# The cell scan of an LSTM recurrence writes to PSUM, and one VectorE operation changes places

## The chip, the core and the metric

The kernel runs on one core of a Trainium2 chip. The metric is the device time of one execution in microseconds (us). The core has TensorE (PE in the profile, its weight loads PEld), VectorE (DVE), ScalarE (ACT), GpSimd (POOL) and SyncE (SP, which only issues DMAs here). Each engine runs its own queue of instructions in order; they meet at semaphores. SBUF is the large on-chip memory, PSUM the small one (here 8 banks of 512 float32 columns on 128 partitions) into which TensorE writes its sums.

## The reference

Four stages in a row on x of shape (4, 256, 128): a conditioned hyperbolic block, a causal multi-head attention, an LSTM over the 256 positions, and a feed-forward layer. The change is in the LSTM alone:

```python
def step(carry, xw_t):                     # 256 steps, one after the other
    prev_h, prev_c = carry
    a = xw_t + prev_h @ Wh                 # (4, 128) @ (128, 512)
    i = sigmoid(a[:, :H]); f = sigmoid(a[:, H:2*H]); o = sigmoid(a[:, 2*H:3*H])
    g = tanh(a[:, 3*H:])
    next_c = f * prev_c + i * g
    next_h = o * tanh(next_c)
    return ((next_h, next_c), next_h)
...
x = x + ffn(lstm(x, cond_1024, Wx, Wh, b))
```

A batch has only four sequences, so every step works on 128 partitions (the hidden units) by a few columns (gates times batch).

## The kernel before

**Layout.** All products with the inputs (Wx) are made ahead, for 32 steps at a time: a chunk. There are 8 chunks (`STEPS` is 32). The accumulators of chunk c stand in PSUM bank 6 or 7, by turns (`bank[:, 6 + (t // STEPS) % 2, ...]`), 16 columns for each step: four gates by batch of four. While chunk c is worked off in one of the two banks, the other one lies idle until step 27 of the chunk; in steps 27 to 31 `inputs_of` fills it for chunk c + 1 (`INPUTS_AT`), where its first matmul starts the sums of the bank afresh.

**One step of the recurrence** goes around the engines like this:

1. TensorE adds h of the step before times Wh to the 16 columns: 12 small matmuls at L1783. h is kept as two float16 parts (`h_off`, and `h_low` for what its rounding leaves), and so is Wh (`wha`, `whb`). Eight matmuls take `h_off` (they wait for `h_ready`), the last four take `h_low` (they wait for `hb_ready`).
2. ScalarE takes tanh of the 16 columns out of PSUM (L832, `gates_act`), into a strided buffer in SBUF, `gates`.
3. VectorE makes the new cell state with one scan over 24 columns (L1391, `c_new`). For each batch element the scan runs through 6 positions, and the sixth is c. It writes to `cell_out`, a buffer in SBUF (`small` in the profile's names).
4. ScalarE takes tanh of the four columns of c (L834, `th_act`).
5. VectorE multiplies it by the output gate into `h_off` (L1402, `h_ready`) and makes `h_low` with a second scan (L1404, `hb_ready`), which reads `h_off` and so waits for `h_ready`.

VectorE has three more small operations in each step. L1393 prepares the output gate. L1397, called the guard below, copies c into the operands of the next step's scan with one bit set, so that it can't be zero; it waits for `c_new` and signals `c_kept`. L1408 takes the reciprocal of what the guard wrote (waits for `c_kept`, signals `c_inverse`), and the next scan waits for it.

**What lies beside it.** Attention of the next chunks, the rest of the hyperbolic block's second half and the feed-forward layer of finished chunks are threaded into the same queues behind each step, at steps written out by hand: `PLAN`, `FFN_STEPS`, and the strings `VEC_GAP` (VectorE work between L1393 and the guard), `VEC_REST`, `ACT_REST` and `PE_REST` (work behind the step). None of these tables changes.

Of the kernel before, what the change touches and what calls it, by code (L numbers as in the profile page):

```python
# [23 lines left out]
ALU = mybir.AluOpType  # L24
ACT = mybir.ActivationFunctionType
# [4 lines left out]
I32 = mybir.dt.int32  # L30

B, S, D, H = 4, 256, 128, 16
# [54 lines left out]
STEPS = 32  # L87
# [5 lines left out]
C_SCALE = 2.0 ** -9  # L93
C_LEAST = 2.0 ** -63
C_LEAST_BITS = 0x20000000
CW = 6
# [5 lines left out]
def adaln_attention_lstm_ffn(nc, x, cond, w_q, b_q, w_k, b_k, w_v, b_v, w_o, b_o, w_f1, b_f1, w_f2, b_f2,  # L102
                             w_ada, b_ada, W_dq, W_uq, W_dkv, W_uk, W_uv, W_o, Wx, Wh, b_g, w1, b1, w2, b2, out):
    with ExitStack() as ctx:
        def sb(name, shape, dt=F32):
            return ctx.enter_context(nc.sbuf_tensor(name, shape, dt))

        def ps(name, shape, dt=F32):
            return ctx.enter_context(nc.psum_tensor(name, shape, dt))

        def sem(name):
            return ctx.enter_context(nc.semaphore(name))
# [97 lines left out]
        cell_out = small[:, 0:2 * CW * B // TILES, :].rearrange("p k t -> p (k t)").rearrange("p (k b s) -> p k b s", k=2, b=B)  # L210
        cell_in1, cell_in0, gate_o = gates[:, :, 0], gates[:, :, 1], gates[:, :, 2, :, 0]
        gates_out = [bass.AP(hn, 3 * k * B * CW + 3, [[3 * TILES * H, P], [(B - 1) * CW + 4, 2], [B * CW - 1, 2], [CW, B]]) for k in range(2)]
        h_fac = sb("h_fac", [P, 2, B, 3])
# [10 lines left out]
        bank = ps("bank", [P, 8, 512])  # L224
# [104 lines left out]
        c_new = sem("c_new")  # L329
        o_ready = sem("o_ready")  # L330
        c_kept = sem("c_kept")
        c_inverse = sem("c_inverse")
        th_act = sem("th_act")
# [4 lines left out]
        x_biased = sem("x_biased")  # L338
        y_ready = sem("y_ready")
        stored = [sem("stored_even"), sem("stored_odd")]  # L340

        block = ctx.enter_context(nc.Block())

# [101 lines left out]
        def attending(t):  # L445
            for c in range(1, CHUNKS):
                if PLAN[c]["co"] <= t <= PLAN[c]["ot"]:
                    yield c
# [5 lines left out]
        def feeding(t):  # L454
            for p, t0 in enumerate(FFN_STEPS):
                feed = FEED_LATE if p == LAST - 1 else FEED
                if 0 <= t - t0 <= feed["result"]:
                    yield p, t - t0, feed
# [7 lines left out]
        def go_on(chain, table, t):  # L466
            for _ in range(int(table[t]) if t < len(table) else 0):
                next(chain)

        @block.sync  # L470
        def _(sp):
# [47 lines left out]
            for k in range(2):  # L519
                sp.wait_ge(stored[k], 16 * sum(c % 2 == k for c, _, _ in PIECES))  # L520
# [67 lines left out]
        def _(act):  # L588
# [228 lines left out]
            def gelu(p, fs=range(FC)):  # L817
                c, a, z = PIECES[p]
                if fs[0] == 0:
                    act.wait_ge(ff_mm, p + 1)  # L820
                    if 2 <= p < LAST:
                        act.wait_ge(y_mm, p - 1)
                for f in fs:
                    nc.scalar.activation(gel[:, c % 2, f, a:z], bank[:, c % 2, f * P + a:f * P + z], ACT.Gelu,  # L824
                                         scale=1.0 / A_SCALE, bias=b1s[:, f:f + 1]).then_inc(gel_ready, 1)

            for t in range(S):
                k = t % 2
                src = bank[:, 6 + (t // STEPS) % 2, (t % STEPS) * GW:(t % STEPS + 1) * GW]

                act.wait_ge(gates_mm, t + 1)
                nc.scalar.activation(gates_out[k], src.rearrange("p (u v b) -> p u v b", u=2, v=2), ACT.Tanh, scale=1.0 / A_SCALE).then_inc(gates_act, 1)  # L832
                act.wait_ge(c_new, t + 1)
                nc.scalar.activation(h_fac[:, k, :, 1], cell_out[:, k, :, 5], ACT.Tanh, scale=1.0 / C_SCALE).then_inc(th_act, 1)  # L834
                for c in attending(t):
                    attend(c, t)
                if t == FFN_STEPS[0]:
                    nc.scalar.preload_act_table_set(GELU)
                go_on(second, ACT_REST, t)
                for p, i, feed in feeding(t):  # L840
                    for j in range(2):
                        if i == feed["gelu"][j]:
                            gelu(p, range(2 * j, 2 * j + 2))
# [3 lines left out]
        def _(vec):  # L847
# [14 lines left out]
            V = nc.vector  # L862
# [523 lines left out]
            for t in range(S):  # L1386
                k = t % 2
                vec.wait_ge(gates_act, t + 1)
                if t:
                    vec.wait_ge(c_inverse, t)  # L1390
                V.tensor_tensor_scan(cell_out[:, k].rearrange("p b s -> p (b s)"), cell_in0[:, k].rearrange("p b s -> p (b s)"),  # L1391
                                     cell_in1[:, k].rearrange("p b s -> p (b s)"), 0.0, ALU.mult, ALU.add).then_inc(c_new, 1)
                V.tensor_scalar(h_fac[:, k, :, 2], gate_o[:, k], 1.0, 0.5 * H_SCALE, ALU.add, ALU.mult).then_inc(o_ready, 1)  # L1393
                go_on(second, VEC_GAP, t)
                if t < S - 1:
                    vec.wait_ge(c_new, t + 1)
                    V.tensor_scalar(cell_in0[:, 1 - k, :, 5].bitcast(I32), cell_out[:, k, :, 5].bitcast(I32), C_LEAST_BITS, None,  # L1397
                                    ALU.bitwise_or).then_inc(c_kept, 1)

                vec.wait_ge(th_act, t + 1)  # L1400
                vec.wait_ge(o_ready, t + 1)
                V.tensor_tensor(h_off[:, t, :, 2], h_fac[:, k, :, 2], h_fac[:, k, :, 1], ALU.mult).then_inc(h_ready, 1)  # L1402
                vec.wait_ge(h_ready, t + 1)
                V.tensor_tensor_scan(h_low[:, t].rearrange("p b s -> p (b s)"), h_fac[:, k].rearrange("p b s -> p (b s)"),  # L1404
                                     h_off[:, t].rearrange("p b s -> p (b s)"), 0.0, ALU.mult, ALU.subtract).then_inc(hb_ready, 1)
                if t < S - 1:
                    vec.wait_ge(c_kept, t + 1)
                    V.reciprocal(cell_in0[:, 1 - k, :, 3], cell_in0[:, 1 - k, :, 5]).then_inc(c_inverse, 1)  # L1408
                for c in attending(t):
                    attend(c, t)  # L1410
                go_on(second, VEC_REST, t)
                if t in BIASED:
                    c = BIASED.index(t)
                    if c == 0:
                        vec.wait_ge(ld_b2, 16)
                    go(V.tensor_tensor(x_tb[:, c, :], x_tb[:, c, :], b2_rows, ALU.add), x_biased)
                for p, i, feed in feeding(t):
                    if i == feed["result"]:
                        result(p)
# [3 lines left out]
        def _(pe):  # L1423
# [266 lines left out]
            def first_inputs(c, gs, t0, t1):  # L1690

                acc = bank[:, 6 + c % 2, :].rearrange("p (t g b) -> p t g b", g=4, b=B)
                for g in gs:
                    ins = T.matmul(acc[:, t0:t1, g, :], wox[:, g, :], oT[:, c * P + t0 * B:c * P + t1 * B], start=False, stop=True, skip_group_check=True)
                return ins
# [80 lines left out]
            for t in range(S):  # L1776
                acc = bank[:, 6 + (t // STEPS) % 2, (t % STEPS) * GW:(t % STEPS + 1) * GW]
                if t:
                    pe.wait_ge(h_ready, t)

                def add(w, h):
                    for g in range(4):
                        ins = T.matmul(acc[:, g * B:(g + 1) * B], w[:, g, :], h, start=False, stop=True, skip_group_check=True)  # L1783
                    return ins

                if t:
                    add(wha, h_off[:, t - 1, :, 2])
                    add(whb, h_off[:, t - 1, :, 2])
                    pe.wait_ge(hb_ready, t)
                    add(wha, h_low[:, t - 1, :, 2]).then_inc(gates_mm, 1)  # L1790
                for c in attending(t):
                    attend(c, t)
                go_on(second, PE_REST, t)
                if t < 4:
                    pe.wait_ge(gates_act, t + 1)
                    first_inputs(0, (t,), SOON, STEPS)
                if t % STEPS in INPUTS_AT and t < S - STEPS:
                    inputs_of(t // STEPS + 1, range(*INPUTS_AT[t % STEPS]))
                for p, i, feed in feeding(t):
                    for f in range(FC):  # L1800
                        if i == feed["up"][f]:
                            ffn_up(p, range(f, f + 1))
                    if i == feed["wo"]:
                        ffn_down(p, range(0, 1))
                    for f in range(FC):
                        if i == feed["down"][f]:
                            ffn_down(p, range(f + 1, f + 2))
# [26 lines left out]
```

## Time and profile before

| | us |
|---|---|
| median of three runs | 537.12 (535.47 to 537.22) |
| the profiled execution | 536.99 |
| its span in the profile | 535.0 |
| first and last cell scan start in the span | 145.4 and 528.6 |

The span begins with the first instruction and ends with the last; 1.99 us of the profiled execution lie outside it. The recurrence fills the span from 145.4 us on, 256 steps. A page of the profile groups instructions by source line, engine and shape, with the mean duration of one. The timeline gives each instruction's start and duration in the order of time. The chain of waits goes back from the last instruction, at each step to what released it.

### The profile page before, as it was taken

Reading aid. Unit: us, or ns where it says so; the run is one execution under the profiler, and the core shown is the slowest. Engines: PE = TensorE matmul, PEld = TensorE weight load, DVE = VectorE, ACT = ScalarE, POOL = GpSimd, SP = SyncE. Lnnn points to the kernel's source line nnn. Section 1 sums busy time; section 2 is a strip of 40 time slices with the busy share of each in tenths; the row PEclk is TensorE's granted clock in tenths of the full one; section 3 lists DMA queues with packets and bytes.
Section 4 is the critical chain, followed back from the end, with each engine's and each line's share of the span. In section 5 each row is a group of like instructions: output and inputs, shape, how many; then the busy total and the mean of one; then the engine's idle time right before and its main releaser. Section 6 shows DMA issues by size and latency. Waiting matters only on the chain.

```text
span 535.0 us, 16653 instructions
## 1 busy us (share of the span) xinstructions
PE 401.8 (75%) x6231; PEld 300.9 (56%) x6231; DVE 390.9 (73%) x2234; ACT 246.8 (46%) x940; POOL 24.1 (5%) x42
## 2 busy tenths in 40 slices
PE   2655867595786799995679787887986786977975
PEld 2325645364565576784457564664764565655753
DVE  7987547539598887878878868778878886655653
ACT  1377866553435346335344434434533434423432
POOL 5000700040000000000000000000000000000000
PEclk9767986598555555555555555555555555555555
DMA  6500000000000000000000000000000000000000
GB/s 198 138 0 1 5 1 2 1 1 1 1 2 2 4 1 3 2 2 2 3 2 2 3 3 1 4 3 1 2 5 2 1 3 1 13 7 1 12 11 7
DMA packets 9340, 6.07 MB, mean 11 GB/s; under 512 B 1988, under 2 KB 8620, under 8 KB 9260
## 3 DMA queue, kind: packets, MB, share of 16 engines
q1 hardware_dynamic: 8076, 4.09, 2.8%
q8 instruction: 49, 0.80, 0.6%
q10 hardware_dynamic: 1184, 0.92, 0.5%
q14 instruction: 31, 0.25, 0.2%
HBM read 4.48 MB, written 0.52 MB: 9 GB/s over the span
## 4 chain that ended last, share of the span: by engine, by line
PE 51%; DVE 25%; ACT 16%; issue 7%; DMA 1%; DVEq 0%; ACTq 0%
PE bank L1783 20%; PE bank L1609 8%; DVE small L1391 6%; ACT h_fac L834 5%; ACT hn L832 5%; DVE vaug L1402 4%; PE bank L1772 3%; PE bank L1682 3%; PE bank L1560 2%; PE bank L1686 2%; PE bank L1586 2%; PE bank L1659 2%; PE bank L1513 1%; PE bank L1756 1%; ACT p_mla L782 1%
## 5 line engine op out<-in xcount | busy, mean ns | idle before, releaser
L1783 PE MATMUL bank<-vaug,wha 128*128 128x4 f16 x2040 | 124.1, 169 | 71.3 <-DVE vaug L1402 68.6
L1783 PEld LDWEIGHTS bank<-vaug,wha 128*128 128x128 f16 x2040 | 95.1, 106 | 138.2 <-DVE vaug L1402 136.0
L832 ACT ACTIVATE hn<-bank 128x16 f32<-128x16 f32 x256 | 51.1, 199 | 148.1 <-PE bank L1783 145.6
L1391 DVE TENSOR_TENSOR_SCAN small<-hn 128x24 f32<-128x24 f32 x256 | 53.0, 207 | 63.5 <-ACT hn L832 59.6
L834 ACT ACTIVATE h_fac<-small 128x4 f32<-128x4 f32 x256 | 53.8, 210 | 72.0 <-DVE small L1391 72.0
L1783 PE MATMUL bank<-vaug,whb 128*128 128x4 f16 x1020 | 62.7, 166 | 0.0
L1402 DVE TENSOR_TENSOR vaug<-h_fac 128x4 f16<-128x4 f32 x256 | 43.4, 169 | 18.3 <-ACT h_fac L834 0.8
L1404 DVE TENSOR_TENSOR_SCAN vaug<-h_fac,vaug 128x12 f16<-128x12 f32 x256 | 46.8, 183 | 8.9
L1609 PE MATMUL bank<-kT,qz 32*128 32x32 f32 (+7 forms) x256 | 51.1, 530 | 0.8 <-ACT kT L801 0.4
L1783 PEld LDWEIGHTS bank<-vaug,whb 128*128 128x128 f16 x1020 | 46.8, 104 | 0.0
L1397 DVE TENSOR_SCALAR hn<-small 128x4 int32<-128x4 int32 x255 | 43.7, 171 | 0.0
L1408 DVE RECIPROCAL hn<-hn 128x4 f32<-128x4 f32 x255 | 41.3, 162 | 0.0
L782 ACT ACTIVATE p_mla<-bank,mx 128x32 f32<-128x32 f32 (+7 forms) x128 | 39.5, 372 | 1.8 <-DVE mx L1326 1.8
L1393 DVE TENSOR_SCALAR h_fac<-hn 128x4 f32<-128x4 f32 x256 | 36.9, 144 | 0.0
L1336 DVE STREAM_TRANSPOSE pt_mla<-p_mla 128x192 f32<-128x192 f32 (+5 forms) x96 | 32.0, 348 | 1.3 <-PE bank L1631 0.6
L1609 PEld LDWEIGHTS bank<-kT,qz 32*128 32x128 f32 x256 | 30.2, 314 | 2.6 <-ACT kT L801 0.8
L1631 PE MATMUL bank<-vbd,pt_mla 128*32 128x36 f32 x1152 | 27.7, 257 | 3.7 <-DVE pt_mla L1336 1.7
L1772 PE MATMUL bank<-w2s,ta 128*128 128x128 f32 (+2 forms) x72 | 26.5, 480 | 0.4 <-ACT ta L824 0.4
L1326 DVE TENSOR_REDUCE mx<-bank 128x2 f32<-128x320 f32 (+7 forms) x48 | 25.1, 530 | 1.9 <-PE bank L1614 1.9
L1631 PEld LDWEIGHTS bank<-vbd,pt_mla 128*32 128x32 f32 x1152 | 21.0, 157 | 6.0 <-DVE pt_mla L1336 5.3
L1492 PE MATMUL bank<-qS,kS 32*128 32x128 f16 x256 | 11.8, 238 | 15.2 <-ACT q_sq L661 8.1
L1492 PEld LDWEIGHTS bank<-qS,kS 32*128 32x128 f16 x256 | 6.7, 100 | 20.8 <-ACT q_sq L661 10.2
(298 smaller groups left out, 670.9 us busy)
## 6 DMA issues: line engine op xcount, KB each, us to landing
x_tm<-in_x ACTq DMA_DIRECT2D x1, 512.0 KB, 5.2
x_tb<-in_x SPq DMA_DIRECT2D x4, 128.0 KB, 2.7
wf<-in_L_cond_w_f SPq DMA_DIRECT2D x2, 256.0 KB, 3.4
out_y<-tb SPq DMA_DIRECT2D x7, 64.0 KB, 1.9
ada_w<-in_L_cond_w_ada SPq DMA_DIRECT2D x1, 384.0 KB
ada_b<-in_L_cond_b_ada ACTq DMA_DIRECT2D x1, 384.0 KB, 5.8
wx<-in_L_cond_Wx SPq DMA_DIRECT2D x2, 128.0 KB
wh<-in_L_cond_Wh SPq DMA_DIRECT2D x2, 128.0 KB, 2.6
```

Source lines behind the costliest of these rows:

```text
L782: ins = nc.scalar.activation(p_mla[:, m % 2, i * n:(i + 1) * n], bank[:, at, i * n:(i + 1) * n], ACT.Exp, bias=mx[:, m % 2, i:i + 1])
L832: nc.scalar.activation(gates_out[k], src.rearrange("p (u v b) -> p u v b", u=2, v=2), ACT.Tanh, scale=1.0 / A_SCALE).then_inc(gates_act, 1)
L834: nc.scalar.activation(h_fac[:, k, :, 1], cell_out[:, k, :, 5], ACT.Tanh, scale=1.0 / C_SCALE).then_inc(th_act, 1)
L1391: V.tensor_tensor_scan(cell_out[:, k].rearrange("p b s -> p (b s)"), cell_in0[:, k].rearrange("p b s -> p (b s)"), cell_in1[:, k].rearrang ...
L1397: V.tensor_scalar(cell_in0[:, 1 - k, :, 5].bitcast(I32), cell_out[:, k, :, 5].bitcast(I32), C_LEAST_BITS, None, ALU.bitwise_or).then_inc(c ...
L1402: V.tensor_tensor(h_off[:, t, :, 2], h_fac[:, k, :, 2], h_fac[:, k, :, 1], ALU.mult).then_inc(h_ready, 1)
L1404: V.tensor_tensor_scan(h_low[:, t].rearrange("p b s -> p (b s)"), h_fac[:, k].rearrange("p b s -> p (b s)"), h_off[:, t].rearrange("p b s ...
L1408: V.reciprocal(cell_in0[:, 1 - k, :, 3], cell_in0[:, 1 - k, :, 5]).then_inc(c_inverse, 1)
L1609: T.matmul(bank[:, at, i * n:(i + 1) * n], qz[rows, c % 2, bs[i]].rearrange("p j t -> p (j t)"), kT[rows, bs[i], 0:n], start=(i == 0), sto ...
L1631: ins = T.matmul(bank[32 * b:32 * b + 32, 5, g * GROUP * VW:(g + 1) * GROUP * VW], pt_mla[:, place, i * n + kb * STEPS:i * n + (kb + 1) * ...
L1772: ins = T.matmul(y, gel[:, c % 2, i - 1, a:z], w2s[:, i - 1, :], start=False, stop=(i == FC), **at)
L1783: ins = T.matmul(acc[:, g * B:(g + 1) * B], w[:, g, :], h, start=False, stop=True, skip_group_check=True)
```

## The change

Three edits. A function `cell_of(t)` says where the cell scan of step t writes and where c is read: in steps 27 to 31 of the first seven chunks the old SBUF buffer, in all other steps 24 columns of the PSUM bank (6 or 7) that isn't in use for the current chunk's gates, at column 0 or 32 by turns. The tanh of c on ScalarE and the guard on VectorE read it there. The guard stands behind the product of `h_off` and ahead of the scan of `h_low`, and has no wait of its own any more. TensorE waits for `c_kept` ahead of the first matmul of `inputs_of` in step 27.

```diff
+        def cell_of(t):
+            if t % STEPS >= STEPS - 5 and t < S - STEPS:
+                return cell_out[:, t % 2]
+            other = bank[:, 6 + (t // STEPS + 1) % 2, (t % 2) * 32:(t % 2) * 32 + B * CW]
+            return other.rearrange("p (b s) -> p b s", s=CW)
...
-                nc.scalar.activation(h_fac[:, k, :, 1], cell_out[:, k, :, 5], ACT.Tanh, scale=1.0 / C_SCALE).then_inc(th_act, 1)
+                nc.scalar.activation(h_fac[:, k, :, 1], cell_of(t)[:, :, 5], ACT.Tanh, scale=1.0 / C_SCALE).then_inc(th_act, 1)
...
-                V.tensor_tensor_scan(cell_out[:, k].rearrange("p b s -> p (b s)"), cell_in0[:, k].rearrange("p b s -> p (b s)"),
+                V.tensor_tensor_scan(cell_of(t).rearrange("p b s -> p (b s)"), cell_in0[:, k].rearrange("p b s -> p (b s)"),
                                      cell_in1[:, k].rearrange("p b s -> p (b s)"), 0.0, ALU.mult, ALU.add).then_inc(c_new, 1)
                 V.tensor_scalar(h_fac[:, k, :, 2], gate_o[:, k], 1.0, 0.5 * H_SCALE, ALU.add, ALU.mult).then_inc(o_ready, 1)
                 go_on(second, VEC_GAP, t)
-                if t < S - 1:
-                    vec.wait_ge(c_new, t + 1)
-                    V.tensor_scalar(cell_in0[:, 1 - k, :, 5].bitcast(I32), cell_out[:, k, :, 5].bitcast(I32), C_LEAST_BITS, None,
-                                    ALU.bitwise_or).then_inc(c_kept, 1)
 
                 vec.wait_ge(th_act, t + 1)
                 vec.wait_ge(o_ready, t + 1)
                 V.tensor_tensor(h_off[:, t, :, 2], h_fac[:, k, :, 2], h_fac[:, k, :, 1], ALU.mult).then_inc(h_ready, 1)
+                if t < S - 1:
+                    V.tensor_scalar(cell_in0[:, 1 - k, :, 5].bitcast(I32), cell_of(t)[:, :, 5].bitcast(I32), C_LEAST_BITS, None,
+                                    ALU.bitwise_or).then_inc(c_kept, 1)
                 vec.wait_ge(h_ready, t + 1)
...
+                if t % STEPS == STEPS - 5 and t < S - STEPS:
+                    pe.wait_ge(c_kept, t)
```

Of the 256 steps, 35 (five in each of seven chunks) keep the buffer in SBUF and 221 use PSUM.

On VectorE, a step of chunk 7 stood like this before; the cell scan is printed here as SCALAR_TENSOR_TENSOR, `small` is the buffer in SBUF:

```order
1970 L1391 SCALAR_TENSOR_TENSOR small<-hn 128x24 [waits c_inverse,gates_act]
1971 L1393 TENSOR_SCALAR h_fac<-hn 128x4
1972 L1397 TENSOR_SCALAR hn<-small 128x4 [waits c_new]
1973 L1402 TENSOR_TENSOR vaug<-h_fac 128x4 [waits o_ready,th_act]
1974 L1404 SCALAR_TENSOR_TENSOR vaug<-h_fac,vaug 128x12 [waits h_ready]
1975 L1408 RECIPROCAL hn<-hn 128x4 [waits c_kept]
```

The same step of the changed kernel, on VectorE, with line numbers of that kernel:

```order
1970 L1397 SCALAR_TENSOR_TENSOR bank<-hn 128x24 [waits c_inverse,gates_act]
1971 L1399 TENSOR_SCALAR h_fac<-hn 128x4
1972 L1404 TENSOR_TENSOR vaug<-h_fac 128x4 [waits o_ready,th_act]
1973 L1406 TENSOR_SCALAR hn<-bank 128x4
1974 L1409 SCALAR_TENSOR_TENSOR vaug<-h_fac,vaug 128x12 [waits h_ready]
1975 L1413 RECIPROCAL hn<-hn 128x4 [waits c_kept]
```

The scan's output is PSUM (`bank`), and the guard has moved one place down, past the product, and lost its wait for `c_new`.

On TensorE, at a chunk's step 27, these rows stand around the first matmul that fills the other bank, before:

```order
1404 L1783 MATMUL bank<-vaug,wha 128x4 [waits hb_ready]
1405 L1783 MATMUL bank<-vaug,wha 128x4 x3
1406 L1680 MATMUL bank<-gate_cols,bg_rows 128x512
1407 L1783 MATMUL bank<-vaug,wha 128x4 [waits h_ready]
1408 L1783 MATMUL bank<-vaug,wha 128x4 x3
```

And in the changed kernel, on TensorE at the same place:

```order
1404 L1788 MATMUL bank<-vaug,wha 128x4 [waits hb_ready]
1405 L1788 MATMUL bank<-vaug,wha 128x4 x3
1406 L1685 MATMUL bank<-gate_cols,bg_rows 128x512 [waits c_kept]
1407 L1788 MATMUL bank<-vaug,wha 128x4 [waits h_ready]
1408 L1788 MATMUL bank<-vaug,wha 128x4 x3
```

Nothing has moved there; the matmul at L1685 has one wait more.

## Rows read from the trace of the kernel before

**Rows 1.** The page: the chain that ended last, share of the span by engine.

```profile
PE 51%; DVE 25%; ACT 16%; issue 7%; DMA 1%; DVEq 0%; ACTq 0%
```

**Rows 2.** Chain of waits, one step of chunk 7: start us, us, what.

```profile
482.88 0.22 DVE small L1391
...
483.12 0.22 ACT h_fac L834
...
483.36 0.18 DVE vaug L1402
...
483.58 0.50 PE bank L1783 x12
...
484.11 0.21 ACT hn L832
```

**Rows 3.** Timeline of that step: start us, us, engine, line, operation, count [idle before].

```profile
483.12 0.17 DVE L1397 TENSOR_SCALAR hn<-small 128x4 int32<-128x4 int32 x1
...
483.56 0.18 DVE L1404 TENSOR_TENSOR_SCAN vaug<-h_fac,vaug 128x12 f16<-128x12 f32 x1
483.66 0.16 DVE L1408 RECIPROCAL hn<-hn 128x4 f32<-128x4 f32 x1
...
483.80 0.19 PEld L1783 LDWEIGHTS bank<-vaug,wha 128*128 128x128 f16 x4
...
484.34 0.21 DVE L1391 TENSOR_TENSOR_SCAN small<-hn 128x24 f32<-128x24 f32 x1 [0.52 <-ACT hn L832]
```

**Rows 4.** Groups by line: busy us, mean ns of one, idle before and releaser.

```profile
L834 ACT ACTIVATE h_fac<-small 128x4 f32<-128x4 f32 x256 | 53.8, 210 | 72.0 <-DVE small L1391 72.0
L1391 DVE TENSOR_TENSOR_SCAN small<-hn 128x24 f32<-128x24 f32 x256 | 53.0, 207 | 63.5 <-ACT hn L832 59.6
L832 ACT ACTIVATE hn<-bank 128x16 f32<-128x16 f32 x256 | 51.1, 199 | 148.1 <-PE bank L1783 145.6 <-PE bank L1694 0.6
```

**Rows 5.** The same view, ScalarE from PSUM (`bank`) and from SBUF.

```profile
L644 ACT ACTIVATE x_tm<-bank 128x512 f32<-128x512 f32 x2 | 1.1, 594 | 0.0
L635 ACT ACTIVATE w_mla<-bank 128x256 f32<-128x256 f32 x1 | 0.4, 376 | 0.0
L639 ACT ACTIVATE wx<-wx 128x256 f32<-128x256 f32 x1 | 0.4, 412 | 0.0
```

**Rows 6.** The same view, VectorE with an input in PSUM and without.

```profile
L1384 DVE TENSOR_TENSOR tb<-bank,x_tb 128x128 f32<-128x128 f32 x7 | 1.8, 260 | 0.0
L1416 DVE TENSOR_TENSOR x_tb<-x_tb,mask 128x128 f32<-128x128 f32 x8 | 2.1, 263 | 0.0
...
L1326 DVE TENSOR_REDUCE mx<-bank 128x4 f32<-128x512 f32 x4 | 2.6, 659 | 0.0
L945 DVE TENSOR_REDUCE small<-tb 128x4 f32<-128x512 f32 x2 | 1.3, 673 | 0.0
L1359 DVE RECIPROCAL rdm<-bank 128x16 f32<-128x16 f32 x8 | 1.9, 231 | 0.5 <-PE bank L1631 0.5
L1110 DVE RECIPROCAL sm<-sm 128x4 f32<-128x4 f32 x4 | 0.7, 178 | 0.1
```

**Rows 7.** Timeline of VectorE in a step with work in the gap.

```profile
165.59 0.16 DVE L1190 SCALAR_TENSOR_TENSOR sm<-sm 128x4 f32<-128x4 f32 x1
165.66 0.17 DVE L1397 TENSOR_SCALAR hn<-small 128x4 int32<-128x4 int32 x1
```

**Rows 8.** Timeline, first and last step in which TensorE is late.

```profile
159.93 0.17 DVE L1402 TENSOR_TENSOR vaug<-h_fac 128x4 f16<-128x4 f32 x1
160.22 0.16 PEld L1783 LDWEIGHTS bank<-vaug,wha 128*128 128x128 f16 x3 [0.20 <-DVE vaug L1402]
...
419.28 0.17 DVE L1402 TENSOR_TENSOR vaug<-h_fac 128x4 f16<-128x4 f32 x1
419.66 0.19 PEld L1783 LDWEIGHTS bank<-vaug,wha 128*128 128x128 f16 x4 [0.46 <-DVE vaug L1402]
```

**Rows 9.** Stretches: us, busy of PE, PEld, DVE, ACT, POOL, clock, DMA.

```profile
145.40:529.30 383.90, 307.28 (x5079) 232.93 (x5078) 292.21 (x1870) 164.11 (x743) 0.00 (x0) 0.50 0.01 3
```

## The prediction

> **What bounds the kernel now.** I read the chain that ended last first [rows 1]: PE 51%, DVE 25%, ACT 16%, so no single engine bounds the kernel; a loop through three of them does. Next I took the chain of waits in a quiet step of chunk 7 [rows 2]. One turn goes scan 482.88, tanh of c 483.12, product 483.36, twelve matmuls 483.58, tanh of the gates 484.11, next scan 484.34 [rows 2, 3]. That is 1.46 us a turn, all of it latency of tiny instructions. Each link is the duration of one instruction and about 0.03 us until the next one starts: the tanh of c takes 0.210 us [rows 4] and its follower starts 0.24 us after it. Whatever shortens or lengthens one of these five links moves the step by the same amount.
>
> Two steps in a row are not always that short. In 29 steps, counted in the timeline, the first weight load of the recurrence comes over 0.26 us after the product's start, where a quiet step has 0.22; the first such step is t=9 (159.93 to 160.22), the last t=181 (419.28 to 419.66) [rows 8]. There TensorE is still at work on attention when h is ready, and what the loop gains or loses before that point vanishes in its backlog. 28 of the 29 are among the 221 PSUM steps, so 193 steps pass a change of the scan or the tanh on in full. In some 25 others, counted the same way, VectorE's attention work holds up the next scan; they count in full, since that work is queued behind the product and moves with it. TensorE's granted clock is 0.50, the lower level (1.2 GHz), through the whole recurrence [rows 9], so a few ns more or less of idle time have nothing to switch.
>
> **The change, part by part.**
>
> *ScalarE's tanh of c reads PSUM.* The same engine has both kinds in each step: the tanh of the gates, 128x16 out of PSUM, takes 199 ns; the tanh of c, 128x4 out of SBUF, 210 ns [rows 4]. The source with four times the columns is 11 ns shorter. A column costs (594 - 376) / 256 = 0.85 ns on ScalarE [rows 5], so 12 columns fewer are 10 ns, and the new tanh comes to 189 ns: 21 ns saved. Bounds: 11 ns if the columns cost nothing at this size; 36 ns by the larger pair of 256 columns, 412 out of SBUF against 376 out of PSUM [rows 5]. I take 21, since rows 4 are the same function at nearly the same size.
>
> *VectorE's scan writes PSUM.* No row shows VectorE writing there, so this is the open price. It counts in full: the tanh of c waits for the scan in all 256 steps [rows 4]. The nearest rows are VectorE's reads of PSUM [rows 6]. A tensor_tensor of 128 columns takes 260 ns with one input in PSUM and 263 with none; a reduction of 512 columns 659 against 673. One pair goes the other way: a reciprocal of 16 strided columns from PSUM takes 231 ns, one of 4 columns from SBUF 178; 12 columns at about 1 ns account for 12 to 14 of the 53, which leaves 39. So the bounds are -14 and +39 ns. I take 0, by the tensor_tensor pair, whose -3 is the smallest difference; both ends go into the range.
>
> The Trainium skill, VectorE: DVE Perf Modes, in its section on the TRN2 errata, gives a fixed cost for an operation by its source: VectorE 58 cycles from SBUF but 120 from PSUM at 0.96 GHz, ScalarE 224 from SBUF and 172 from PSUM at 1.2 GHz. If VectorE's figure held for its write as well, the scan would cost an estimated 65 ns more and the tanh 43 less, 21 ns a step the wrong way, and the sum would be +4.1 us in place of my minus. The trace bears out ScalarE's half (36 ns in the pair of rows 5) and not VectorE's for reads (rows 6); for a write no row decides.
>
> *The guard behind the product.* Before, it starts with the tanh of c (483.12), takes 0.17 us and is done before the product at 483.36 [rows 2, 3]: it was hidden, and taking it from there gains nothing. Its new place is a hole as well. The low scan starts 0.20 us after the product (483.36 to 483.56), because it waits for the product's result [rows 2, 3]. Independent small operations on VectorE follow one another in 0.07 us (165.59 to 165.66) [rows 7], so guard and low scan can be issued 0.07 and 0.14 us after the product, and the low scan still finds its semaphore the last to come. The guard would be done 0.07 + 0.17 = 0.24 us after the product; the reciprocal that waits for it starts at 0.30 (483.66), so it isn't moved either. The cost is nothing, and the cover is 0.06 us. If that is gone, every ns shows: the low scan, 183 ns long by its row, ends at 483.74 and the third group of weights is loaded at 483.80 [rows 3], about 0.05 us later, the same distance as from the product's end to the first group (483.53 to 483.58). TensorE has no slack there for a late low part.
>
> *The smaller parts.* The dropped wait for `c_new` saves nothing, since the product's wait for the tanh comes later anyway. TensorE's new wait for `c_kept` in step 27 asks for the guard of the step before; that guard stands ahead of the low scan in VectorE's queue, and TensorE has just waited for that scan's semaphore, so it is satisfied: 0, in seven places. What is queued behind that waiting matmul (the next step's L1783) is then not held either. The guard's source in PSUM is hidden as the guard is. No DMA, table or attention step moves.
>
> *Sum.* 193 x (0 - 21 ns) = -4.1 us. From the profiled execution, 536.99 us (span 535.0 and 1.99 outside it), that gives 532.9. This execution lies 0.13 below the median of the runs, 537.12, from which the same sum gives 533.1; I forecast 533.0.
>
> **The rivals.**
>
> *The write is quicker too.* For: every pair of rows 6 but one has PSUM a little ahead. Against: those are reads. At -14 ns for the scan and 21 saved on the tanh, 193 x 35 ns = 6.8 us, so 530.2; with 36 for the tanh 193 x 50 = 9.7, so 527.3.
>
> *What the tanh saves the scan loses.* A scan 15 to 25 ns longer leaves the loop as it is: 537.0. For: the reciprocal pair of rows 6 shows that some small VectorE operation on PSUM costs more. Against: it is a strided read, and the scan writes a contiguous stretch.
>
> *Slower: the scan's result lands late.* The place is the link from scan to tanh of c, 0.24 us in rows 2. At the upper bound of 39 ns the net is +18 ns, 193 x 18 = +3.5 us, so 540.5. It decides from about 29 ns on (21 saved, and 8 more to be seen as 1.6 us over 193 steps). Against it stand three of four comparisons; the rule of the Trainium skill's VectorE page cited above, its errata section, is this case with a higher price.
>
> *The low scan is held by the guard.* If the guard's read of PSUM kept VectorE's queue closed for longer than the 0.06 us of cover, the low scan would start late. Were it to run only once the guard has ended, 0.24 + 0.03 against 0.20, that would be some 70 ns in 193 steps, +13.5 us; with the tanh's 4.1 back, 546.4. Rows 7 speak against it: small operations overlap there to more than half.
>
> *The change doesn't do what it says* can't well be: the order of instructions shows the scan on the PSUM bank and the guard one place down.
>
> **How the numbers follow.** A measurement of this kernel can tell about 0.3%, 1.6 us, from no change, which is 8 ns over 193 steps. Forecast (532.9, spread 531.5 to 535): 0.45. Write quicker too: 0.15. Cancelled: 0.20. Scan lands late: 0.16. Low scan held: 0.04. Faster is the first two, 0.60; the same 0.20; slower the last two, 0.20. For the range, 529.0 takes in all but the far end of the second case, and 540.0 most of the scan that lands late; outside lie 0.04 below, about 0.08 of the late scan above, and the held low scan, 0.16 in all. Since cases of both signs hold chances, the likeliest one's own range is 531.5 to 535.
>
> **What would show each step right or wrong.** In the profile of the changed kernel: the tanh of c with a mean near 189 ns in the PSUM steps and 210 in the other 35; the cell scan's start to the tanh's start still 0.24 us in PSUM steps (0.28 would be the late landing, 0.22 the quicker write); the guard 0.07 us behind the product and the low scan still 0.20 behind it; the third group's weights 0.44 us after the product; a quiet step of 1.45 us against 1.46; the steps 27 to 31 of a chunk unchanged, which makes them a control inside the same trace. The prediction is wrong if the link from scan to tanh moves by more than some 10 ns, or the low scan comes later than 0.21 us after the product.

## The result, and the profile after

The changed kernel took 529.17 us as the median of its first four runs (528.99 to 533.43) against 537.04 before (535.47 to 537.22, four runs), a ratio of 0.989 with a 95% interval of 0.985 to 0.993. Six more runs beside eleven of the kernel before gave 532.51 against 537.45, a ratio of 0.990 (0.987 to 0.993). The profiled execution took 528.99 us, its span 526.8. The forecast was 533.0 us in a range of 529.0 to 540.0: the direction was right, the first median lay just inside the low end, the second beside the forecast. Where the two medians differ is told below; it isn't in the change.

The chain that ended last, on the page of the profile after, has hardly another mix than before [rows 1]:

```profile
PE 52%; DVE 23%; ACT 17%; issue 6%; DMA 1%; DVEq 0%; ACTq 0%
```

One turn of the loop in a quiet step of chunk 7, in the chain of waits (start us, us, what), answers to [rows 2]:

```profile
479.88 0.23 DVE bank L1397
...
480.13 0.18 ACT h_fac L840
...
480.34 0.18 DVE vaug L1404
...
480.57 0.50 PE bank L1788 x12
...
481.09 0.21 ACT hn L838
...
481.33 0.23 DVE bank L1397
```

From scan to scan it is 1.45 us here, 1.46 before. The scan's piece has grown from 0.22 to 0.23 us, the tanh's piece has shrunk from 0.22 to 0.18. The groups by line, with mean durations in ns, show both, and they show the 35 steps that stayed in SBUF (`small`) beside the 221 that moved to PSUM (`bank`); they answer to [rows 4]:

```profile
L1397 DVE TENSOR_TENSOR_SCAN bank<-hn 128x24 f32<-128x24 f32 x221 | 47.7, 216 | 56.7 <-ACT hn L838 54.0
L840 ACT ACTIVATE h_fac<-bank 128x4 f32<-128x4 f32 x221 | 38.9, 176 | 64.2 <-DVE bank L1397 64.2
L840 ACT ACTIVATE h_fac<-small 128x4 f32<-128x4 f32 x35 | 7.4, 210 | 9.8 <-DVE small L1397 9.8
L1397 DVE TENSOR_TENSOR_SCAN small<-hn 128x24 f32<-128x24 f32 x35 | 7.2, 207 | 6.2 <-ACT hn L838 5.5
```

The tanh of c takes 176 ns out of PSUM and 210 out of SBUF: 34 ns less. The scan takes 216 into PSUM and 207 into SBUF: 9 ns more. The tanh of the gates, which didn't change, takes 199 as before. A quiet step is one that neither TensorE's nor VectorE's other work holds up. Over all steps, by the starts in the timeline, the median from scan to tanh went from 241 to 250 ns, from tanh to product from 243 to 208, and the quiet PSUM step from 1.467 to 1.440 us. The quiet SBUF steps, the control inside the trace, went from 1.467 to 1.465.

The timeline of the same step shows the moved guard (L1406) in the hole between product and low scan; it answers to [rows 3]:

```profile
480.34 0.17 DVE L1404 TENSOR_TENSOR vaug<-h_fac 128x4 f16<-128x4 f32 x1 [0.17 <-ACT h_fac L840]
480.42 0.16 DVE L1406 TENSOR_SCALAR hn<-bank 128x4 int32<-128x4 int32 x1
480.55 0.18 DVE L1409 TENSOR_TENSOR_SCAN vaug<-h_fac,vaug 128x12 f16<-128x12 f32 x1
...
480.64 0.16 DVE L1413 RECIPROCAL hn<-hn 128x4 f32<-128x4 f32 x1
...
480.78 0.19 PEld L1788 LDWEIGHTS bank<-vaug,wha 128*128 128x128 f16 x4
```

The guard starts 0.08 us behind the product, the low scan still 0.20 to 0.21 behind it, the reciprocal 0.30, and the third group of weights 0.44. Nothing behind the product has moved.

**Where 8 us came from when the loop gave 5.** The cell scans of the profile after (count; duration min/median/max; first and last start):

```profile
L1397 DVE TENSOR_TENSOR_SCAN bank<-hn x221: 199/217/218, 142.2 to 520.3; 128x24 f32<-128x24 f32 x111
```

The recurrence lasted 520.3 - 142.2 = 378.1 us, against 528.6 - 145.4 = 383.2 before: 5.1 us. The other 3.2 us lie ahead of its first step, where no instruction was changed. What differs there is the granted clock. The stretch from 100 to 125 us, columns as in [rows 9], of the kernel before and then of the kernel after:

```profile
100.00:125.00 25.00, 21.95 (x168) 16.59 (x169) 11.21 (x41) 14.19 (x42) 6.60 (x12) 0.81 0.00 1
```

```profile
100.00:125.00 25.00, 20.91 (x173) 15.94 (x169) 13.10 (x51) 14.26 (x46) 6.63 (x12) 0.93 0.01 2
...
142.20:521.10 378.90, 306.20 (x5079) 232.59 (x5078) 269.59 (x1870) 157.00 (x742) 0.00 (x0) 0.50 0.01 4
```

The clock is the last figure but two of a row, as a share of the upper level. TensorE had the upper of its two levels (2.4 GHz) for a larger part of this busy stretch in the profiled execution after, 0.93 against 0.81 on the mean. Through the recurrence both run at the lower level, 0.50 (the second row, and [rows 9]). The first experiments ask whether that belongs to the change.

### The profile page after: what moved, and what is told of

Read it like the earlier page. It is cut to its first block, busy times and chain, and to the rows that moved or that the text cites. A ratio compares the mean times of both kernels' runs of the same rounds, so it can differ in the third digit from the quotient of the medians.

```text
span 526.8 us, 16653 instructions
## 1 busy us (share of the span) xinstructions
PE 398.6 (76%) x6231; PEld 299.0 (57%) x6231; DVE 367.0 (70%) x2234; ACT 239.8 (46%) x940; POOL 24.4 (5%) x42
## 4 chain that ended last, share of the span: by engine, by line
PE 52%; DVE 23%; ACT 17%; issue 6%; DMA 1%; DVEq 0%; ACTq 0%
PE bank L1788 20%; PE bank L1614 8%; DVE bank L1397 6%; ACT hn L838 5%; ACT h_fac L840 5%; DVE vaug L1404 4%; PE bank L1777 3%; PE bank L1687 3%; PE bank L1691 2%; PE bank L1591 2%; PE bank L1565 2%; PE bank L1664 2%; ACT p_mla L788 2%; PE bank L1518 2%; PE bank L1761 1%
## 5 line engine op out<-in xcount | busy, mean ns | idle before, releaser
L1397 DVE TENSOR_TENSOR_SCAN bank<-hn 128x24 f32<-128x24 f32 x221 | 47.7, 216 | 56.7 <-ACT hn L838 54.0
L840 ACT ACTIVATE h_fac<-bank 128x4 f32<-128x4 f32 x221 | 38.9, 176 | 64.2 <-DVE bank L1397 64.2
L1409 DVE TENSOR_TENSOR_SCAN vaug<-h_fac,vaug 128x12 f16<-128x12 f32 x256 | 46.8, 183 | 0.3
L1399 DVE TENSOR_SCALAR h_fac<-hn 128x4 f32<-128x4 f32 x256 | 40.3, 157 | 0.0
L1406 DVE TENSOR_SCALAR hn<-bank 128x4 int32<-128x4 int32 x220 | 34.6, 157 | 0.1
```

The costliest lines, as they stand in the source:

```text
L840: nc.scalar.activation(h_fac[:, k, :, 1], cell_of(t)[:, :, 5], ACT.Tanh, scale=1.0 / C_SCALE).then_inc(th_act, 1)
L1397: V.tensor_tensor_scan(cell_of(t).rearrange("p b s -> p (b s)"), cell_in0[:, k].rearrange("p b s -> p (b s)"), cell_in1[:, k].rearrange("p ...
```

## The experiments

**The kernel before, again.** No edit.

> The kernel before, unchanged, for the spread of its own executions and for what lies ahead of the recurrence. In the two profiles the first cell scan came at 145.4 us before and at 142.2 us after the change, though no instruction differs up to there; the granted clock of the stretch 100 to 125 us was 0.81 and 0.93. Theory (loop only, 5.1 us; the other 3.2 us are which stretches ahead of the recurrence got the high clock): some executions of this kernel lie 2 to 4 us under the others, with a mean clock near 0.579 instead of 0.573, and the ratio is 1.00. Rival (the change itself moves the start of the recurrence): all executions stay at 535.4 to 537.3 with the clock at 0.573.

Twelve executions lay at 533.6 to 539.1 us with a median of 537.02, ratio 1.000 (0.997 to 1.003). In the 63 further executions of this kernel that ran beside the experiments, the time goes mostly by the mean granted clock: at 0.578 13 executions, 533.4 to 534.4 us; at 0.573 and 0.574 25, 536.4 to 537.5; at 0.572 15, 538.1 to 539.3; the other ten lie between 534.9 and 539.4. The theory holds and the rival falls: between the two ends, which go with the clock, lie some 5 us with nothing changed in the kernel. The profile of this run started its recurrence at 145.1 us and spent 527.8 - 145.1 = 382.7 us in it:

```profile
L1391 DVE TENSOR_TENSOR_SCAN small<-hn x256: 191/208/210, 145.1 to 527.8; 128x24 f32<-128x24 f32 x128
```

**The kernel after, again.** No edit.

> The changed kernel again, beside more runs of the kernel before. Over 29 executions the kernel before lay at 533.8 to 539.4 us, by how long the high clock was granted ahead of the recurrence; three of the first four executions of the changed kernel had the longest grant (mean clock 0.579). Theory (the change is worth the 5.0 us that the recurrence lost, the rest of the first 8 us was the draw of the clock): median 531.5 to 532.5, spread 528.8 to 534.5, ratio 0.989 to 0.992, recurrence 378.1 us within 0.4. Rival (the changed program starts the recurrence earlier as a rule): median at 529.2 again, ratio 0.985 to 0.987.

```profile
L1397 DVE TENSOR_TENSOR_SCAN bank<-hn x221: 200/216/218, 146.7 to 524.6; 128x24 f32<-128x24 f32 x111
```

The recurrence took 524.6 - 146.7 = 377.9 us, but this time it began at 146.7. The median was 532.51, as the theory had it. Sorted by the mean clock, the ten executions of the changed kernel are 529.0 to 529.4 us at 0.579 (four), 532.1 to 533.1 at 0.574 (three), 533.4 and 533.5 at 0.572, and one of 532.5 at 0.570. Against the groups of the kernel before at 0.578, at 0.573 and 0.574, and at 0.572, that is some 4.7, 4.5 and 5.2 us less. So the change is worth about 5 us, 0.9%; the first median of 529.17 had three of its four executions at the highest mean clock.

**The guard alone.** The order of the changed kernel, all cells in SBUF:

```diff
         def cell_of(t):
-            if t % STEPS >= STEPS - 5 and t < S - STEPS:
+            if t >= 0:
                 return cell_out[:, t % 2]
```

> The guard stands behind the product as in the changed kernel, but the cell scan writes to SBUF in all 256 steps. Theory (the whole gain of the loop comes from PSUM, the guard's place is worth nothing in a quiet step): a quiet step stays at 1.467 us, first to last cell scan 383.2 us within 0.5, ratio 0.999 to 1.001 apart from what happens ahead of the recurrence. Rival (the guard ahead of the product was in the way): a quiet step of 1.44 to 1.46 us, 2 us or more gained in the recurrence.

```profile
L1397 DVE TENSOR_TENSOR_SCAN small<-hn x256: 191/208/210, 142.3 to 525.2; 128x24 f32<-128x24 f32 x128
```

525.2 - 142.3 = 382.9 us, between the 383.2 and 382.7 of the kernel before; a quiet step is 1.466 us; ratio 1.001 (0.998 to 1.003). The place of the guard is worth nothing while c stands in SBUF. No run leaves the guard at its old place with c in PSUM, where it and the tanh of c, which start together at 483.12 [rows 2, 3], would read one bank at the same time; what that does stays open. The same profile started its recurrence at 142.3 us, with all cells in SBUF, so the early start doesn't come from PSUM either.

**The write alone.** The scan writes to PSUM, ScalarE reads the buffer in SBUF:

```diff
-                nc.scalar.activation(h_fac[:, k, :, 1], cell_of(t)[:, :, 5], ACT.Tanh, ...
+                nc.scalar.activation(h_fac[:, k, :, 1], cell_out[:, k, :, 5], ACT.Tanh, ...
```

> The cell scan writes to PSUM as in the changed kernel, but the tanh of c reads the old SBUF buffer in all steps (so h is computed from a cell state that isn't the new one). It prices the write alone. Theory (write +9 ns, read -35 ns, and the two add up): tanh at 210 ns, scan 217, scan to tanh 0.250 us, quiet step 1.476 us, the recurrence 2 us longer than the 383.2 us of the kernel before. Rival (part of the 9 ns is only there when ScalarE reads the same bank next): scan to tanh under 0.245 us and no loss.

```profile
L1397 DVE TENSOR_TENSOR_SCAN bank<-hn x221: 198/217/218, 147.4 to 531.9; 128x24 f32<-128x24 f32 x111
```

The scan took 217 ns and the tanh 210; scan to tanh was 250 ns. The recurrence took 384.5 us, 1.3 more than in the kernel before (2 expected) and 1.6 more than with the guard alone; ratio to the kernel before 1.003 (1.000 to 1.006). A quiet PSUM step was 1.472 us (1.476 expected) against 1.461 in this trace's SBUF steps, which are 0.005 us shorter than in the other traces; why, is open. The price of the write is there without any reader in PSUM, so the rival falls.

**The read alone.** The scan and the guard stay in SBUF, the tanh reads the idle bank:

```diff
-                V.tensor_tensor_scan(cell_of(t).rearrange("p b s -> p (b s)"), ...
+                V.tensor_tensor_scan(cell_out[:, k].rearrange("p b s -> p (b s)"), ...
...
-                    V.tensor_scalar(cell_in0[:, 1 - k, :, 5].bitcast(I32), cell_of(t)[:, :, 5].bitcast(I32), ...
+                    V.tensor_scalar(cell_in0[:, 1 - k, :, 5].bitcast(I32), cell_out[:, k, :, 5].bitcast(I32), ...
```

> The cell scan writes to SBUF in all steps and the guard reads it there; the tanh of c reads four columns of the idle PSUM bank (so h is computed from other numbers). It prices the read alone. Theory: tanh 176 ns in the 221 steps, quiet step 1.432 us, the recurrence 7 us shorter than 383.2 us. Rival (the read is only quick because VectorE has just written there, or the product gives part back): tanh near 189 ns or a quiet step above 1.44 us.

```profile
L840 ACT ACTIVATE h_fac<-bank x221: 175/176/178, 146.9 to 523.5; 128x4 f32<-128x4 f32 x111
L840 ACT ACTIVATE h_fac<-small x35: 209/210/211, 187.5 to 477.5; 128x4 f32<-128x4 f32 x35
```

Its scans start from 146.7 to 523.2 us: 376.5 us of recurrence, 6.4 less than with the guard alone, a quiet PSUM step of 1.430 us; the whole execution's ratio was 0.986 (0.982 to 0.989). The rival, a tanh of 189 ns, falls: the read is just as quick where VectorE hasn't written. The two halves add up: +1.6 - 6.4 = -4.8, and the whole change against the guard alone is 378.1 - 382.9 = -4.8. The gain is ScalarE's read, and the write gives a quarter of it back.

**Half the steps.** PSUM in the even chunks only:

```diff
-            if t % STEPS >= STEPS - 5 and t < S - STEPS:
+            if t % STEPS >= STEPS - 5 and t < S - STEPS or t // STEPS % 2:
                 return cell_out[:, t % 2]
```

> The changed kernel with PSUM for the cell only in the even chunks (0, 2, 4, 6: 4 x 27 = 108 steps). Theory (a fixed gain for each step that uses PSUM): quiet steps of 1.440 us in even chunks and 1.465 in odd ones inside one trace, the recurrence about 2.5 us shorter than 383.2 us. Rival (something else in the changed program, not the place of the cell, made the gain): odd and even chunks alike.

In the timeline the medians of quiet steps are 1.439 us in the 108 PSUM steps and 1.466 in the others. The source view of the scan:

```profile
L1397 DVE TENSOR_TENSOR_SCAN small<-hn x148: 198/208/209, 188.1 to 527.9; 128x24 f32<-128x24 f32 x148
L1397 DVE TENSOR_TENSOR_SCAN bank<-hn x108: 199/217/219, 147.3 to 473.5; 128x24 f32<-128x24 f32 x108
```

527.9 - 147.3 = 380.6 us, 2.3 under the guard alone, half of the whole for half the steps; ratio 0.997 (0.994 to 1.000). The gain belongs to each step that uses PSUM.

**One and two more operations in the hole.** After the guard, n times, into a spare buffer:

```diff
                                     ALU.bitwise_or).then_inc(c_kept, 1)
+                    V.tensor_scalar(spare[:, n * t + i, :].bitcast(I32), cell_of(t)[:, :, 5].bitcast(I32), C_LEAST_BITS, None, ALU.bitwise_or)
```

> The changed kernel with one more operation like the guard (four columns of c from PSUM into a spare buffer) between guard and low scan, in all steps. By the prediction guard and low scan can be issued 0.07 us apart, so the hole of 0.20 us holds the guard with 0.06 us to spare. Theory: with one more the low scan starts 0.21 us after the product in place of 0.20, a quiet step 1.44 to 1.45 us, ratio to the kernel before 0.990 to 0.995. Rival (a read from PSUM holds the queue, and the guard alone fills the hole): low scan at 0.27 us or later, quiet step 1.50 us.

> The same with two more operations. Theory: the low scan starts 0.28 us after the product, 0.075 us late; the third group of weights waits for it and a quiet step takes 1.51 us; 193 steps x 0.075 us = 14 us longer than the changed kernel, 543 us. Rival (TensorE has slack for a late low part): quiet step under 1.46 us.

VectorE's timeline with one more (L1409) in a quiet step, product L1405, guard L1407, low scan L1411:

```profile
500.02 0.17 DVE L1405 TENSOR_TENSOR vaug<-h_fac 128x4 f16<-128x4 f32 x1 [0.17 <-ACT h_fac L841]
500.10 0.16 DVE L1407 TENSOR_SCALAR hn<-bank 128x4 int32<-128x4 int32 x1
500.17 0.15 DVE L1409 TENSOR_SCALAR kS<-bank 128x4 int32<-128x4 int32 x1
500.24 0.17 DVE L1411 TENSOR_TENSOR_SCAN vaug<-h_fac,vaug 128x12 f16<-128x12 f32 x1
```

And with two more (L1409, L1410):

```profile
480.88 0.17 DVE L1405 TENSOR_TENSOR vaug<-h_fac 128x4 f16<-128x4 f32 x1 [0.17 <-ACT h_fac L841]
480.96 0.16 DVE L1407 TENSOR_SCALAR hn<-bank 128x4 int32<-128x4 int32 x1
481.03 0.15 DVE L1409 TENSOR_SCALAR kS<-bank 128x4 int32<-128x4 int32 x1
481.10 0.15 DVE L1410 TENSOR_SCALAR kS<-bank 128x4 int32<-128x4 int32 x1
481.10 0.18 PEld L1791 LDWEIGHTS bank<-vaug,wha 128*128 128x128 f16 x4 [0.61 <-DVE vaug L1405]
481.17 0.17 DVE L1412 TENSOR_TENSOR_SCAN vaug<-h_fac,vaug 128x12 f16<-128x12 f32 x1
```

Guard and spare operations follow one another in 0.07 us, PSUM or not. The low scan starts at a median of 203 ns behind the product with the guard alone, 220 with one more, 288 with two, and the quiet PSUM step goes 1.440, 1.447, 1.514 us. So the hole had about 0.05 us to spare. That 17 ns late cost only 7, and 85 late 74, isn't slack of TensorE: the low scan itself is 9 ns shorter once the product's semaphore is there before its turn comes. Its median is 183 ns in the changed kernel and 174 with one more:

```profile
L1409 DVE TENSOR_TENSOR_SCAN vaug<-h_fac,vaug x256: 173/183/185, 142.9 to 521.0; 128x12 f16<-128x12 f32 x128
```

```profile
L1411 DVE TENSOR_TENSOR_SCAN vaug<-h_fac,vaug x256: 172/174/183, 147.5 to 529.4; 128x12 f16<-128x12 f32 x128
```

So the low scan ends 386 ns behind the product, then 394, then some 463, and the third group of weights is loaded at 440, 448 and 516: it follows the end of the low scan to a ns or two.

With one more the ratio was 0.998 (0.995 to 1.001), not the 0.990 to 0.995 expected, and the recurrence took 528.7 - 146.8 = 381.9 us, 3.8 longer than the changed kernel's. Ten single steps make 2.3 us of that: in them the low scan starts 390 to 470 ns behind the product. The first of them is step 4, where the guard starts 0.32 us behind the product and not 0.08, with nothing to wait for (`issue`):

```profile
153.46 0.17 DVE L1405 TENSOR_TENSOR vaug<-h_fac 128x4 f16<-128x4 f32 x1 [0.17 <-ACT h_fac L841]
153.78 0.17 DVE L1407 TENSOR_SCALAR hn<-bank 128x4 int32<-128x4 int32 x1 [0.15 <-issue]
```

Counted through all of VectorE's instructions in the trace, waits included, these pauses of 0.17 to 0.24 us lie 128 instructions or a multiple of it apart. The kernels before and after have them as well, at the same steps in both traces of each. An added operation per step shifts them to other steps. What the pause is, no run shows. The other 245 steps together lost 1.4 us.

With two more it was 551.9 us, ratio 1.029 (1.025 to 1.033). The recurrence took 396.1 us, 18.0 more than the changed kernel's against the 14 expected: the expectation had left out the 35 SBUF steps, which are late as well and make 2.8, and some 1.0 comes from the pauses. The 543 us expected had moreover started from the 529 us of the changed kernel's first median.

**The price list.** The changed kernel with one operation more per step in the last chunk, on idle engines:

```diff
+                if t >= S - STEPS:          # ScalarE, after the tanh of the gates
+                    n, j = (4, 8, 16, 16)[t % 4], t - (S - STEPS)
+                    nc.scalar.activation(spare[:, j, 0:n], (bank[:, 5, 0:n] if t % 4 < 3 else xT[:, 0:n]), ACT.Tanh, ...)
...
+                    if t % 4 < 2:           # VectorE, after the reciprocal; "to" is PSUM for odd t
+                        V.tensor_tensor_scan(to[:, 0:24] if t % 2 else spare_v[:, j, :], xT[:, 0:24], xT[:, 24:48], ...)
+                    else:
+                        V.tensor_scalar(to[:, 24:28] if t % 2 else spare_v[:, j, 0:4], xT[:, 0:4], ...)
```

> The changed kernel with one idle-time operation more per step in the last chunk, on ScalarE and on VectorE: ScalarE tanh of 4, 8 and 16 columns from PSUM and of 16 from SBUF, VectorE a scan of 24 columns and a tensor_scalar of 4 columns from SBUF into PSUM and into SBUF, all without use. It measures the slope of the tanh and the price of a write. Prediction's step (0.85 ns a column, 189 ns at 4 columns from PSUM): tanh 189, 192, 199 ns. Theory now (the tanh of c was 176 ns): 4 columns near 176, 8 near 184, 16 near 195; SBUF 34 ns over PSUM at 16 columns. VectorE: scan +9 ns into PSUM; tensor_scalar +9 if the price is fixed for each instruction, +1 or 2 if it goes by columns.

The groups by line and shape:

```profile
L844 ACT ACTIVATE kS<-x_tm 128x16 f32<-128x16 f32 x8 | 1.7, 207 | 0.0
L1424 DVE TENSOR_TENSOR_SCAN bank<-x_tm 128x24 f32<-128x24 f32 x8 | 1.5, 186 | 0.0
L1424 DVE TENSOR_TENSOR_SCAN kS<-x_tm 128x24 f32<-128x24 f32 x8 | 1.4, 180 | 0.0
L844 ACT ACTIVATE kS<-bank 128x16 f32<-128x16 f32 x8 | 1.4, 178 | 0.0
...
L844 ACT ACTIVATE kS<-bank 128x4 f32<-128x4 f32 x8 | 1.3, 168 | 0.0
```

On ScalarE 4, 8 and 16 columns out of PSUM took 168, 173 and 178 ns, so 12 columns are worth 10 ns, as the prediction had it, and 16 columns out of SBUF cost 29 ns more. But a plain tanh of 16 columns takes 178 ns where the gates' tanh takes 199. On VectorE the scan is 6 ns dearer into PSUM; a tensor_scalar of 4 columns took 143 ns into SBUF and 155 into PSUM. These two come from the source view:

```profile
L1426 DVE TENSOR_SCALAR kS<-x_tm x8: 140/143/144, 482.4 to 522.6; 128x4 f32<-128x4 f32 x8
L1426 DVE TENSOR_SCALAR bank<-x_tm x7: 153/155/167, 483.8 to 518.3; 128x4 f32<-128x4 f32 x7
```

Four columns cost more than 24, so the write's price goes by the instruction and doesn't grow with the columns.

**The form of the tanh.** The same, with eight forms of tanh by turns; the ones that decide:

```diff
+                        nc.scalar.activation(dst[:, :, :, 0:16:4], z.rearrange("p (u v b) -> p u v b", u=2, v=2), ACT.Tanh, ...)   # scattered
...
+                        nc.scalar.activation(room[:, 0:16], z, ACT.Tanh, ...)                                                     # plain
...
+                        nc.scalar.activation(bank[:, 5, 256 + 4 * (j // 8):260 + 4 * (j // 8)], bank[:, 5, 0:4], ACT.Tanh, ...)  # PSUM to PSUM
```

> The changed kernel with one tanh more per step on idle ScalarE in the last chunk, of eight forms by turns, none of them used: from PSUM 16 columns into a scattered target like that of the gates (groups of four with a gap between the elements), 16 into 16 adjacent columns, 16 into groups of four adjacent columns, 16 with one stride; 4 columns read with a stride of six, as c is; 4 written with a stride of three; 4 from PSUM to PSUM; 4 from SBUF. It asks why the gates' tanh takes 199 ns where a plain one of 16 columns took 178. Theory (the layout of its target costs the 21 ns, so it was a false yardstick for the tanh of c): the scattered form near 195 ns, the plain one 178. Rival (something of the place in the step costs them, such as waking up from a wait): scattered and plain alike, near 178. The strided forms of 4 columns: 172 to 176 against 168. PSUM to PSUM: 150 to 168.

```profile
L860 ACT ACTIVATE kS<-x_tm 128x4 f32<-128x4 f32 x4 | 0.8, 197 | 0.0
L858 ACT ACTIVATE kS<-bank 128x16 f32<-128x16 f32 x4 | 0.8, 193 | 0.0
L846 ACT ACTIVATE kS<-bank 128x16 f32<-128x16 f32 x4 | 0.8, 193 | 0.0
L854 ACT ACTIVATE bank<-bank 128x4 f32<-128x4 f32 x4 | 0.7, 184 | 0.0
L848 ACT ACTIVATE kS<-bank 128x16 f32<-128x16 f32 x4 | 0.7, 178 | 0.0
L856 ACT ACTIVATE kS<-bank 128x16 f32<-128x16 f32 x4 | 0.7, 178 | 0.0
L852 ACT ACTIVATE kS<-bank 128x4 f32<-128x4 f32 x4 | 0.7, 169 | 0.0
L850 ACT ACTIVATE kS<-bank 128x4 f32<-128x4 f32 x4 | 0.7, 168 | 0.0
```

L846 has a scattered target like that of the gates, though with a stride of four elements where the gates have six, L858 a target with one stride of four: 193 ns both. L848 is plain and L856 writes groups of four adjacent elements: 178 both. So gaps between the elements of the target cost 15 ns at 16 columns, and that is most of the 21 between 199 and 178. At 4 columns neither a stride in the source (L850) nor in the target (L852) costs anything. The remaining 6 to 8 ns (199 against 193, 176 against 168) may be the price of standing directly behind a wait, as the low scan's 183 against 174 ns are on VectorE; for ScalarE that wasn't tested by itself, nor was the gates' stride of six. Each form ran four times, in one execution.

## Why the prediction was right

**The loop.** That each link counts in full held: the links changed by +9 and -35 ns, the quiet step by -27. The count of steps held as well: 193 x 26 ns = 5.0 us, and the recurrence lost 4.6 to 5.3 between the two traces of the kernel before (383.2 and 382.7 us) and the two of the kernel after (378.1 and 377.9). All 220 intervals that follow a PSUM step would have given 5.7; the steps in which TensorE is late anyway swallowed the rest. Taken by the first of each step's twelve weight loads, those are 28 in either trace, where the prediction says 29, and 27 of them are PSUM steps; 220 - 27 is 193 again. Step by step, these 27 gained 0.02 us in sum between the two profiles, the others 27 ns in the median.

**The sum.** -4.1 us forecast, some -5.0 measured. That it came so near is in part luck: the tanh's term was 13 ns too small, the scan's 9 ns too favourable, and the two errors cancelled but for some 5 ns. The first median of 529.17 lay inside the range by 0.17 us only, because of the clock ahead of the recurrence.

**The tanh out of PSUM.** The term was mis-sized: 21 ns taken, 34 measured, inside the bounds of 11 to 36. The step of the argument that failed is "the same function at nearly the same size". The columns were right; the yardstick was not, because a tanh of 16 columns pays 15 ns for a scattered target like the gates', and one of four columns doesn't. The pair of 256 columns in rows 5, with plain layouts on both sides, was nearly right with 36.

**The scan into PSUM.** Taken as 0 from VectorE's reads, measured +9 in its place and +6 idle, within -14 to +39. It lay just under the 10 ns that the prediction had set as its sign of being wrong. Reads were no proxy even for the sign. The guard at the same place took 157 ns out of PSUM and 165 out of SBUF, so reading saves 8 where writing costs 9:

```profile
L1406 DVE TENSOR_SCALAR hn<-bank x220: 155/157/166, 142.8 to 519.4; 128x4 int32<-128x4 int32 x110
L1406 DVE TENSOR_SCALAR hn<-small x35: 163/165/172, 183.6 to 474.7; 128x4 int32<-128x4 int32 x35
```

The Trainium skill, VectorE: DVE Perf Modes, in its section on the TRN2 errata, gives 120 cycles in place of 58 for a source in PSUM, an estimated 65 ns more. The guard's rows contradict it for a read, and no case of a write here came near it. The prediction's "three of four comparisons" against a late landing are two of the three pairs that rows 6 show.

**The guard and the waits.** Right as told: worth nothing where it was, and the hole holds it, with 0.05 us to spare against the 0.06 predicted, since the guard starts 0.08 us behind the product and not 0.07. That TensorE has no slack for a late low part was right too: the third group of weights moved with the end of the low scan. The wait for `c_kept` cost nothing that the traces show.

**The rivals.** A late landing of 39 ns and a scan that eats the tanh's gain fell with the write-only run. "The write is quicker too" named a gain near the measured one for a wrong reason: the whole surplus came from the read. The low scan held by the guard fell with the low scan's start, 203 ns behind the product as before.

**What the prediction didn't see.** It took the span of one execution as a fixed base and put 0.13 us between it and the median. The kernel before, unchanged, took from 533.4 to 539.4 us, mostly by the clock ahead of the recurrence. That spread is as large as the effect; it and not the change made the first difference 8 us instead of 5. Nor did it see the pauses of VectorE, which took back 0.2 us here and 2.3 us in the run with one more operation.

## What to carry to other kernels

In a loop of tiny dependent instructions, choose for each intermediate the memory that is cheap for the engine that reads it, and add both ends of the exchange: here ScalarE's read saves 34 ns and VectorE's write costs 9. A duration from the same engine is a yardstick only if the layout of source and target match too, gaps between elements included. And where executions differ by the clock of an unchanged stretch, compare the stretch that was changed, from its first instruction to its last, before the ends of the span.

## What the hardware showed that I had not expected

- ScalarE writes 16 elements with gaps in SBUF in 193 ns and 16 adjacent ones, or four groups of four, in 178.
- ScalarE from PSUM to PSUM took 184 ns for 4 columns against 168 from PSUM to SBUF. Source and target lay in one bank; two banks weren't tried. The Trainium skill, ScalarE: Activation LUTs, in Step-by-step: what each stage is for, has ScalarE's way to PSUM as the faster one; for this small tanh the trace says the opposite by 16 ns.
- VectorE is 8 ns quicker reading four columns of PSUM than of SBUF and 12 slower writing them.
- The same scan of 12 columns on VectorE lasts 183 ns when it has to wait for its semaphore and 174 when the semaphore is there already.
- VectorE pauses for 0.17 to 0.24 us at places that lie 128 of its instructions, or a multiple of it, apart. It shows only where the engine wasn't waiting anyway.
- One and the same program got a mean clock of 0.565 to 0.578 and took 533.4 to 539.4 us; in the profiles the clock differs ahead of the recurrence and is 0.50 all through it. What decides the draw is open.
